# A state-space block and a top-k router on one core: another order of loads, biases and product steps at the end

## The chip, the cores and the metric

The kernel runs on one core of a Trainium2 chip. Its engines are TensorE (PE, matrix products), VectorE (DVE), ScalarE (ACT), GpSimd (POOL) and SyncE (SP); each has its own in-order instruction stream, and SP and ScalarE here also issue DMA transfers, each on a hardware queue of its own. The metric is the device time of one execution in microseconds. All data are fp32.

## The reference, cut to what matters

```python
# x (4, 1024, 1024), ctx (4, 1024, 512)
x = x + tanh(g_xattn) * mamba(ctx, layernorm(x))   # in_proj, conv of 4 taps, state scan over 1024 steps, 16 states, gate
xn = layernorm(x)
# expert-choice router: 16 experts, one shared expert matrix
S = softmax(xn @ router_w + router_b)              # (4096 tokens, 16)
G, idx = top_k(S.T, 256)                           # each expert takes its 256 best tokens
out = xn[idx] @ expert_w + expert_b                # (16, 256, 1024)
y = zeros.at[idx].add(G * out)
return x + tanh(g_ffn) * y
```

All experts use the same matrix, so a token's output is `x2 + c * (xn @ expert_w + expert_b)` with `c = tanh(g_ffn)` times the sum of the token's scores over the experts that picked it.

## The kernel before, in words

The 4096 tokens are eight halves `h` of 512 tokens (`NC = 8`), each of four tiles of 128 tokens (`TT = 4`). All engines walk through slots `g` of a half; slot tables at the top of the file say at which slot, and how many halves late, each piece of work is issued. A half's state-space part runs first; its second layer norm, logits and expert product follow in the slots of later halves. `LAST = 7`, `LATE = 6` are the two halves whose tail is left when the scans are over; `half(NC, REST)` issues the last eight slots' worth of it, after which the order is written out by hand. The parts that the change touches are these.

**Product.** `product_step` multiplies one 128x128 piece of transposed normed tokens with 512 columns of the expert matrix; eight steps make a unit (half a tile), two units a tile. The weights come in 256 KB pieces through a ring of five places (`wk`, `load_step`). When the scans are over, the space of `bbc` is free, and SP loads the whole matrix into it (`wres`, eight loads of 512 KB). The last twelve units (`units_end`: four of `LATE`, eight of `LAST`) use it, in `product_end_step(j)`, 96 steps. ScalarE copies each finished unit out of PSUM (`unit_end`). The products of tiles 0 to 25 are in DRAM (`prod_dram`), those of tiles 26 to 31 stay on chip (`product_end`), `NBACK = 26`.

**Logits at the end.** TensorE transposes the normed tokens of a tile in two groups of four (`turn_end`), ScalarE and VectorE copy them to SBUF, and `logits_end` adds up 16-column matmuls. Softmax scores of all halves lie in `S_tok`.

**Search.** The scores are transposed to 128 rows (eight halves by 16 experts) of 512. Thirty rounds find the bits of each expert's 256th largest score: VectorE counts scores over a candidate, a 128x1 matmul adds the counts of an expert's rows, VectorE decides the bit. TensorE puts one product step into each round.

**Selection.** `gtm` marks scores above the threshold, `eqm` those equal, a scan counts the equal ones (`cum`), two small matmuls sum over rows, `sele` becomes the mask times the scores, and four matmuls with `seg_of` sum it over the experts: `coef`, one factor per token.

**Draining the tiles.** For each of 32 tiles VectorE adds the bias of the expert (`biased`, 128x1024), then computes `x2 + coef * product` (`finish`); SP stores it. There are `NSLOT = 9` pairs of places for a tile of the product (`pr`) and of `x2` (`x2b`). SP fills them for tiles 0 to 8 before the search (`load_back`). Tiles 9 to 27 are loaded by ScalarE (`load_again`), two tiles after each unit from the seventh on and the others after the last unit; each load waits until the store of the place's tile before has landed. VectorE issues `biased(i + 1)` ahead of `finish(i)`.

Of the kernel before, what the change touches and what calls it, by code (L numbers as in the profile page):

```python
# [6 lines left out]
ALU = mybir.AluOpType  # L7
# [10 lines left out]
E = D // P  # L18
# [69 lines left out]

SLOTTED = 4
NRING, NPIECE = 5, 3  # L90

NSLOT = 9
NBACK = (NC - 1) * TT - 2

# [33 lines left out]
def mamba_moe(nc, x, ctxT, g_xattn, g_ffn, winT, conv_w, conv_b, xpT, dtpT, dt_b, a_log, dvec,  # L128
              router_w, router_b, expert_w, expert_b, consts, row_masks, out):
    with ExitStack() as ctx:  # L130
# [159 lines left out]
        s_sp2 = sem("selection_sums")  # L290
        s_mask = sem("masks_in")
# [7 lines left out]
        s_o1 = sem("product_biased")  # L299
        s_o = sem("tile_done")  # L300
# [47 lines left out]
        def _(sp):  # L348
# [169 lines left out]


# [4 lines left out]
            half(NC, REST)  # L524
            store_unit(LATE, SLOTTED - 1)

            def load_back(i):
                h, t = divmod(i, TT)
                sp.wait_ge(s_pw, 16 * 2 * (i + 1))
                sp.dma_start(pr[i], prod_dram[h, :, t, :]).then_inc(s_ld[i], 16)  # L530
                sp.dma_start(x2b[i], x2_dram[h, :, t, :]).then_inc(s_ld[i], 16)
# [10 lines left out]
            for i in range(NC * TT):  # L542
# [3 lines left out]
                sp.dma_start(out[h, t * P:(t + 1) * P, :], pr[slot] if i < NBACK else product_end[h][t]).then_inc(s_st[slot], 16)  # L546
            for i in range(NSLOT):
                sp.wait_ge(s_st[i], 16 * len(range(i, NBACK, NSLOT)))
# [4 lines left out]
        def _(pe):  # L553
# [93 lines left out]
            def logits_end(h, t):  # L647
                if h == LATE:

                    pe.wait_ge(s_pe, n(h, 2 * TT, SLOTTED))  # L650
# [6 lines left out]
                dst = (pM if h == LATE else pU)[:, t * NX:(t + 1) * NX]  # L657
# [38 lines left out]
            def product_end_step(j):  # L696
# [3 lines left out]
                if j == 0:  # L700
                    pe.wait_ge(s_wres, 16 * E)
                if k == 0:
# [76 lines left out]
            for t in range(1, TT):  # L779
                turn_end(LAST, 2 * t)  # L780
                turn_end(LAST, 2 * t + 1)
                logits_end(LAST, t - 1)
# [9 lines left out]

            for i in range(BITS):
                pe.wait_ge(s_b, 2 + 3 * i + 2)
                pe.matmul(pD[:, 0:1], same_expert, small[:, 0:1], start=True, stop=True).then_inc(s_cnt, 1)
                product_end_step(i)
            pe.wait_ge(s_sel, 3)
            pe.matmul(pD[:, 2:3], same_expert, small[:, 1:2], start=True, stop=True)
            pe.matmul(pD[:, 4:5], earlier, cum[:, T - 1:T], start=True, stop=True).then_inc(s_sp2, 1)
            pe.wait_ge(s_sel, 8)  # L800
            for j in range(TT):
                mm = pe.matmul(pY[:, j * NC:(j + 1) * NC], sele[:, eT(j)], seg_of, start=True, stop=True)
            mm.then_inc(s_sp2, 1)
            for j in range(BITS, len(units_end) * E):
# [3 lines left out]
        def _(act):  # L808
# [120 lines left out]
            def logits_end(h):  # L929
# [5 lines left out]
                else:  # L935
                    nc.scalar.copy(lg[:, 2:4, :].rearrange("p t s -> p (t s)"), pM[:, 2 * NX:TT * NX]).then_inc(s_lga, 2)
# [114 lines left out]
            def load_again(i):  # L1051

                h, t = divmod(i, TT)
                slot = i % NSLOT
# [426 lines left out]
```

## Time and profile before

| | |
|---|---|
| time, median of 3 runs | 2131.61 us (2131.18 to 2132.29) |
| profiled execution, its own time | 2129.65 us |
| its span, first to last instruction | 2127.5 us |
| mean granted TensorE clock | 0.88 |
| moved by DMA | 348.19 MB |

The span runs from the first to the last instruction of the profiled execution; its own time holds in addition what lies around them. Rows give start and duration in us from the span's start. L705 is line 705 of the kernel before. The granted clock is a share of the full 2.4 GHz. Tensors that share space have the name of the space: `bbc` is also the resident expert matrix, `cbc`, `states`, `u` and `sz` the places of tiles, `steps` the expert bias, `szT` the factors `coef`, `states` the masks and scores of the search.

### The profile page before, as it was taken

The numbers are of one execution on the slowest core, as the hardware profiler recorded it, in microseconds if no ns is written. First come the engines' busy times: TensorE is split into PE (matmuls) and PEld (weight loads), VectorE is DVE, ScalarE is ACT, GpSimd is POOL, SyncE is SP. The second block draws the span as 40 slices with busy tenths as digits, with TensorE's granted clock in tenths as the row PEclk, the third lists the DMA queues.
The fourth block names the chain that finished last, engine by engine and source line by source line (L and its number), as shares of the span: only waits on it lengthen the run. The fifth ranks groups of instructions, "written<-read, shape, count | busy, mean of one in ns | idle before, by whom it ended". The sixth has DMA issues, their size and how long they took to land.

```text
span 2127.5 us, 23357 instructions
## 1 busy us (share of the span) xinstructions
PE 1654.1 (78%) x7564; PEld 1082.5 (51%) x7564; DVE 1931.3 (91%) x2055; ACT 1405.6 (66%) x2115; POOL 1736.6 (82%) x758
## 2 busy tenths in 40 slices
PE   7456666678888888888878988889888778778790
PEld 2234444454555555555555555555555555556340
DVE  7988989999999899999999999999999999982667
ACT  3455756787788768786888777876888687742000
POOL 0488989998999999998999999999999999980000
PEclk9678888889999999999999988999999889886995
DMA  9600214133844465345735473537524553355088
GB/s 368 251 26 16 85 62 183 31 125 101 307 130 145 139 228 185 118 155 181 246 115 178 127 283 111 177 111 267 170 89 149 198 198 114 126 186 196 6 311 354
DMA packets 139001, 348.19 MB, mean 164 GB/s; under 512 B 15234, under 2 KB 17794, under 8 KB 129666
## 3 DMA queue, kind: packets, MB, share of 16 engines
q1 hardware_dynamic: 133698, 327.83, 44.4%
q10 hardware_dynamic: 5184, 18.88, 2.3%
q8 instruction: 61, 1.00, 0.2%
q14 instruction: 58, 0.48, 0.1%
HBM read 301.04 MB, written 45.61 MB: 163 GB/s over the span
## 4 chain that ended last, share of the span: by engine, by line
POOL 25%; PE 25%; DVE 19%; issue 15%; ACT 10%; DMA 4%; SPq 0%; DVEq 0%; POOLq 0%; ACTq 0%
POOL states L1366 15%; DVE states L1105 11%; POOL states L1354 8%; PE pY L599 7%; PE pM L693 5%; PE pA L567 4%; ACT pDec L852 4%; DVE states L1090 2%; PE pA L576 2%; DVE u L1080 2%; PE pDec L705 2%; ACT L836 1%; DMA bbc<-bc_scratch 1%; POOL dtub L1345 1%; PE pY L595 1%
## 5 line engine op out<-in xcount | busy, mean ns | idle before, releaser
L1366 POOL TENSOR_TENSOR states<-states,cbc 128x2048 f32<-128x2048 f32 x256 | 1160.5, 4536 | 32.5 <-DVE states L1105 21.8
L852 ACT ACTIVATE pDec<-steps,an 128x512 f32<-128x512 f32 x1024 | 685.1, 687 | 412.8 <-DVE states L1105 408.4
L599 PE MATMUL pY<-con,states 128*128 128x128 f32 x4096 | 587.0, 306 | 185.1 <-POOL states L1366 184.9
L599 PEld LDWEIGHTS pY<-con,states 128*128 128x128 f32 x4096 | 541.3, 160 | 303.3 <-POOL states L1366 242.1
L1105 DVE TENSOR_TENSOR_SCAN states<-pDec,carry,states 128x512 f32<-128x512 f32 x512 | 625.9, 1265 | 25.5 <-ACT pDec L852 24.9
L1105 DVE TENSOR_TENSOR_SCAN states<-pDec,states 128x512 f32<-128x512 f32 x512 | 594.8, 1204 | 37.8 <-ACT pDec L852 37.6
L1354 POOL TENSOR_TENSOR states<-dtub,bbc 128x1024 f32<-128x1024 f32 x192 | 454.3, 2366 | 63.4 <-PE pY L599 50.7
L693 PE MATMUL pM<-wk,xfT 128*128 128x512 f32 x832 | 424.6, 626 | 2.3 <-DMA wk<-in_expert_w 2.3
L1090 DVE TENSOR_TENSOR states<-pU,bbc 128x1024 f32<-128x1024 f32 x320 | 384.9, 1203 | 5.0 <-DMA bbc<-bc_scratch 3.5
L567 PE MATMUL pA<-ctx_sb,winb 128*128 128x512 f32 x448 | 228.4, 657 | 62.7 <-issue 30.1
L693 PEld LDWEIGHTS pM<-wk,xfT 128*128 128x128 f32 x832 | 148.3, 204 | 83.8 <-issue 82.2
L567 PEld LDWEIGHTS pA<-ctx_sb,winb 128*128 128x128 f32 x448 | 91.9, 211 | 184.9 <-issue 140.2
L595 PE MATMUL pY<-ddiag,u 128*128 128x128 f32 x512 | 79.1, 303 | 90.6 <-issue 73.2
L1011 ACT ACT_TABLE_LOAD x109 | 139.8, 1283 | 2.0
L595 PEld LDWEIGHTS pY<-ddiag,u 128*128 128x128 f32 x512 | 71.3, 211 | 130.5 <-issue 112.2
L1080 DVE SCALAR_TENSOR_TENSOR u<-pA,cw,u 128x509 f32<-128x509 f32 x171 | 125.1, 731 | 2.1
L1345 POOL TENSOR_TENSOR dtub<-steps,u 128x512 f32<-128x512 f32 x64 | 81.7, 1277 | 11.8 <-ACT steps L836 11.8
L836 ACT ACT_TABLE_LOAD x64 | 82.1, 1283 | 1.2
L585 PE MATMUL pD<-xpr,dtp 32*128 32x512 f32 x128 | 73.6, 655 | 11.9 <-ACT xfT L900 10.2
L610 PEld LDWEIGHTS pA<-con,sz 128*128 128x128 f32 x256 | 38.5, 168 | 63.5 <-issue 63.5
L864 ACT COPY szT<-pA 128x512 f32<-128x512 f32 x64 | 37.0, 578 | 41.6 <-PE pA L610 41.6
L1113 DVE TENSOR_TENSOR pY<-pY,szT 128x512 f32<-128x512 f32 x64 | 43.4, 678 | 22.7 <-PE pY L599 22.6
(206 smaller groups left out, 1421.5 us busy)
## 6 DMA issues: line engine op xcount, KB each, us to landing
wk<-in_expert_w SPq DMA_DIRECT2D x416, 256.0 KB, 4.3
bbc<-bc_scratch SPq DMA_DIRECT2D x32, 1024.0 KB, 7.3
cbc<-bc_scratch SPq DMA_DIRECT2D x32, 1024.0 KB, 9.4
sz<-in_x SPq DMA_DIRECT2D x34, 512.0 KB, 6.0
xt<-in_x SPq DMA_DIRECT2D x15, 1024.0 KB, 5.6
winb<-in_winT SPq DMA_DIRECT2D x58, 256.0 KB, 2.6
x_scratch<-xt SPq DMA_DIRECT2D x14, 1024.0 KB, 6.0
xr<-x_scratch SPq DMA_DIRECT2D x28, 512.0 KB, 4.0
```

What stands on the lines that cost most here:

```text
L567: mm = pe.matmul(pA[:], win[j % 2][:, part, :], ctx_sb[:, part, :], start=(part == 0), stop=(part == KC - 1))
L595: mm = pe.matmul(pY[:, eT(t)], u[h % 2][:, e, eT(t)], ddiag[:], start=(t == 0), stop=False)
L599: mm = pe.matmul(pY[:, eT(t)], states[g % NST][:, i, eT(t)], ident, start=False, stop=(q == QG - 1 and i == QN - 1 and t == TT - 1), is_tr ...
L693: pe.matmul(pM[:], piece_of(h, 2 * t + k // 4)[:, k % 4, :], wk[:, c % NRING, :], start=(k == 0), stop=(k == E - 1)).then_inc(s_moe, 1)
L836: nc.scalar.activation(dt[e % 2], pD[:], ACT.Softplus, bias=dtb[:, e:e + 1]).then_inc(s_sp, 1)
L852: nc.scalar.activation(pDec[bank_of(h, k)][:], dt[e % 2], ACT.Exp, scale=an[:, k:k + 1]).then_inc(s_dec, 1)
L1011: nc.scalar.preload_act_table_set(EXP)
L1080: nc.vector.scalar_tensor_tensor(out=dst, in0=bank[:, 0:T - HALO + i], scalar=cw[:, j, i:i + 1], in1=dst, op0=ALU.mult, op1=ALU.add).then_ ...
L1090: nc.vector.tensor_tensor(states[g % NST], spread(pU), bbc[:, QN * q:QN * (q + 1), :], ALU.mult) \
L1105: nc.vector.tensor_tensor_scan(st, pDec[bank_of(h, k)][:], st, 0.0 if h % HB == 0 else carry[:, e, k % NS:k % NS + 1], ALU.mult, ALU.add). ...
L1354: nc.gpsimd.tensor_tensor(states[g % NST], spread(dtu[e % 2]), bbc[:, QN * q:QN * (q + 1), :], ALU.mult) \
L1366: nc.gpsimd.tensor_tensor(st, st, cbc[:, QW * q:QW * (q + 1), :], ALU.mult).then_inc(s_hc, 1)
```

## The change

- SP issues only the first four of the last eight slots (`WK_REST`) before the eight loads of the expert matrix, and with them the last four small weight pieces; before, the eight loads came first.
- The logits of the last two tiles of `LATE` go to the PSUM bank `pDec[2]` and no longer wait for the copy of the unit in `pM`. The second late unit, which uses that bank, waits until they are copied.
- Six of the 96 late product steps (`EARLY = 2` after each pair of `turn_end` of tiles 1 to 3) are issued before the last logits; the search starts with the seventh.
- GpSimd adds the bias to tiles 0 to 8 as they arrive; VectorE adds it to the others only.
- Selection: the two row sums accumulate in one PSUM column; the mask above the threshold is multiplied by the scores on GpSimd, the mask of equal scores on VectorE behind the scan; both are summed by TensorE, four matmuls each.
- Loads of tiles 9 to 27 are issued by SP: after store `i`, from `i = 2` on, it waits for the landing of store `i - 2` and loads tile `i + 7`. ScalarE issues no more loads.

```diff
...
 REST = 8
+EARLY = 2
 SLOTTED = 4
+WK_REST = 4
 NRING, NPIECE = 5, 3
 NSLOT = 9
 NBACK = (NC - 1) * TT - 2
+LAG = 2
 def at(slots, g, h):
...
         s_cnt = sem("counts_summed")
         s_sel = sem("selection_step")
         s_sp2 = sem("selection_sums")
+        s_above = sem("above_threshold")
         s_mask = sem("masks_in")
         s_big = sem("expert_bias_in")
         s_wk = [sem(f"expert_ring{i}_in") for i in range(NRING)]
...
         s_pw = sem("product_written")
         s_ld = [sem(f"tile{i}_back") for i in range(NSLOT)]
         s_o1 = sem("product_biased")
+        s_o1p = sem("product_biased_pool")
         s_o = sem("tile_done")
         s_st = [sem(f"out{i}_written") for i in range(NSLOT + 1)]
...
             for h in range(NC):
                 half(h)
+            half(NC, WK_REST)
             sp.wait_ge(s_bmd, n(NC, len(DVE_GROUPS), 0))
             sp.wait_ge(s_bmp, n(NC, len(POOL_GROUPS), 0))
             for k in range(E):
                 sp.dma_start(wres[:, k, :], expert_w[k * P:(k + 1) * P, :]).then_inc(s_wres, 16)
-            half(NC, REST)
+            for g in range(WK_REST, REST):
+                side(NC, g)
             store_unit(LATE, SLOTTED - 1)
             def load_back(i):
                 h, t = divmod(i, TT)
-                sp.wait_ge(s_pw, 16 * 2 * (i + 1))
-                sp.dma_start(pr[i], prod_dram[h, :, t, :]).then_inc(s_ld[i], 16)
-                sp.dma_start(x2b[i], x2_dram[h, :, t, :]).then_inc(s_ld[i], 16)
+                slot = i % NSLOT
+                wait(sp, s_st[slot], 16 * (i // NSLOT))
+                if i < NBACK:
+                    sp.wait_ge(s_pw, 16 * 2 * (i + 1))
+                    sp.dma_start(pr[slot], prod_dram[h, :, t, :]).then_inc(s_ld[slot], 16)
+                sp.dma_start(x2b[slot], x2_dram[h, :, t, :]).then_inc(s_ld[slot], 16)
             sp.wait_ge(s_hc, n(NC, NP, 0))
...
                 sp.wait_ge(s_o, i + 1)
                 slot = i % NSLOT if i < NBACK else NSLOT
                 sp.dma_start(out[h, t * P:(t + 1) * P, :], pr[slot] if i < NBACK else product_end[h][t]).then_inc(s_st[slot], 16)
+                if i >= LAG and i - LAG + NSLOT < LAST * TT:
+                    load_back(i - LAG + NSLOT)
             for i in range(NSLOT):
                 sp.wait_ge(s_st[i], 16 * len(range(i, NBACK, NSLOT)))
             sp.wait_ge(s_st[NSLOT], 16 * (NC * TT - NBACK))
...
             def logits_end(h, t):
                 if h == LATE:
-                    pe.wait_ge(s_pe, n(h, 2 * TT, SLOTTED))
+                    pe.wait_ge(s_scan, n(NC, NU, 0))
                     pe.wait_ge(s_xfT, n(h, 2 * TT, 2 * t + 2))
                 else:
                     pe.wait_ge(s_bmd, n(NC, len(DVE_GROUPS), 0))
                     pe.wait_ge(s_xfT, n(LAST, 2 * TT, t + 1))
                     pe.wait_ge(s_xfTv, t + 1)
-                dst = (pM if h == LATE else pU)[:, t * NX:(t + 1) * NX]
+                dst = (pDec[2] if h == LATE else pU)[:, t * NX:(t + 1) * NX]
                 pe.matmul(dst, one[:], rb[:], start=True, stop=False)
                 for f in range(2):
                     piece = piece_of(h, 2 * t + f)
...
                 t, hh = divmod(i, 2)
                 if j == 0:
                     pe.wait_ge(s_wres, 16 * E)
+                if unit == 1 and k == 0:
+                    pe.wait_ge(s_lga, n(LATE, TT, TT))
                 if k == 0:
                     pe.wait_ge(s_pe, n(LATE, 2 * TT, SLOTTED + max(unit - len(p_end) + 1, 0)))
...
             for t in range(1, TT):
                 turn_end(LAST, 2 * t)
                 turn_end(LAST, 2 * t + 1)
+                for j in range(EARLY * (t - 1), EARLY * t):
+                    product_end_step(j)
                 logits_end(LAST, t - 1)
             logits_end(LAST, TT - 1)
...
             mm.then_inc(s_srt, 1)
+            first = EARLY * (TT - 1)
             for i in range(BITS):
                 pe.wait_ge(s_b, 2 + 3 * i + 2)
                 pe.matmul(pD[:, 0:1], same_expert, small[:, 0:1], start=True, stop=True).then_inc(s_cnt, 1)
-                product_end_step(i)
+                product_end_step(first + i)
             pe.wait_ge(s_sel, 3)
-            pe.matmul(pD[:, 2:3], same_expert, small[:, 1:2], start=True, stop=True)
-            pe.matmul(pD[:, 4:5], earlier, cum[:, T - 1:T], start=True, stop=True).then_inc(s_sp2, 1)
-            pe.wait_ge(s_sel, 8)
+            pe.matmul(pD[:, 2:3], same_expert, small[:, 1:2], start=True, stop=False)
+            pe.matmul(pD[:, 2:3], earlier, cum[:, T - 1:T], start=False, stop=True).then_inc(s_sp2, 1)
+            pe.wait_ge(s_above, 2)
             for j in range(TT):
-                mm = pe.matmul(pY[:, j * NC:(j + 1) * NC], sele[:, eT(j)], seg_of, start=True, stop=True)
+                pe.matmul(pY[:, j * NC:(j + 1) * NC], gtm[:, eT(j)], seg_of, start=(j == 0), stop=False)
+            pe.wait_ge(s_sel, 6)
+            for j in range(TT):
+                mm = pe.matmul(pY[:, j * NC:(j + 1) * NC], sele[:, eT(j)], seg_of, start=False, stop=(j == TT - 1))
             mm.then_inc(s_sp2, 1)
-            for j in range(BITS, len(units_end) * E):
+            for j in range(first + BITS, len(units_end) * E):
                 product_end_step(j)
         @block.scalar
...
                     act.wait_ge(s_sto, n(h, 1, 0))
                     nc.scalar.copy(lg[:].rearrange("p t s -> p (t s)"), pU[:, 0:TT * NX]).then_inc(s_lga, TT)
                 else:
-                    nc.scalar.copy(lg[:, 2:4, :].rearrange("p t s -> p (t s)"), pM[:, 2 * NX:TT * NX]).then_inc(s_lga, 2)
+                    nc.scalar.copy(lg[:, 2:4, :].rearrange("p t s -> p (t s)"), pDec[2][:, 2 * NX:TT * NX]).then_inc(s_lga, 2)
             def gate_silu(h, part):
                 wait(act, s_zx[part % 2], n(h, 32, 16 * (part // 2 + 1)))
...
             router_exp(LAST)
             scores(LAST)
-            def load_again(i):
-                h, t = divmod(i, TT)
-                slot = i % NSLOT
-                act.wait_ge(s_st[slot], 16 * (i // NSLOT))
-                if i < NBACK:
-                    nc.scalar.dma_start(pr[slot], prod_dram[h, :, t, :]).then_inc(s_ld[slot], 16)
-                nc.scalar.dma_start(x2b[slot], x2_dram[h, :, t, :]).then_inc(s_ld[slot], 16)
-            act.wait_ge(s_pw, 16 * n(LATE, 2 * TT, SLOTTED))
-            act.wait_ge(s_x2w, n(LAST, 32, 0))
-            again = iter(range(NSLOT, (NC - 1) * TT))
             for j in range(len(units_end)):
                 unit_end(j)
-                for _ in range(2 if j > 5 else 0):
-                    load_again(next(again))
-            for i in again:
-                load_again(i)
         @block.vector
         def _(dve):
...
             dve.wait_ge(s_b, 2 + 3 * BITS)
             thf = thr.bitcast(F32)
-            nc.vector.tensor_scalar(gtm, srt, thf, 0.0, ALU.is_gt, ALU.add, accum_out=small[:, 1:2])
+            nc.vector.tensor_scalar(gtm, srt, thf, 0.0, ALU.is_gt, ALU.add, accum_out=small[:, 1:2]).then_inc(s_above, 1)
             nc.vector.tensor_scalar(eqm, srt, thf, None, ALU.is_equal).then_inc(s_sel, 1)
             dve.wait_ge(s_sel, 1)
             nc.vector.tensor_tensor_scan(cum, ones, eqm, 0.0, ALU.mult, ALU.add).then_inc(s_sel, 2)
+            nc.vector.tensor_tensor(eqm, eqm, srt, ALU.mult).then_inc(s_sel, 1)
             dve.wait_ge(s_sp2, 1)
-            nc.vector.tensor_scalar(small[:, 3:4], pD[:, 2:3], -1.0, float(TOPK), ALU.mult, ALU.add).then_inc(s_sel, 1)
-            dve.wait_ge(s_sel, 4)
-            nc.vector.tensor_tensor(small[:, 4:5], small[:, 3:4], pD[:, 4:5], ALU.subtract).then_inc(s_sel, 1)
+            nc.vector.tensor_scalar(small[:, 4:5], pD[:, 2:3], -1.0, float(TOPK), ALU.mult, ALU.add).then_inc(s_sel, 1)
             dve.wait_ge(s_sel, 5)
             nc.vector.scalar_tensor_tensor(out=sele, in0=cum, scalar=small[:, 4:5], in1=eqm,
                                            op0=ALU.is_le, op1=ALU.mult).then_inc(s_sel, 1)
-            dve.wait_ge(s_sel, 6)
-            nc.vector.tensor_tensor(sele, sele, gtm, ALU.add).then_inc(s_sel, 1)
-            dve.wait_ge(s_sel, 7)
-            nc.vector.tensor_tensor(sele, sele, srt, ALU.mult).then_inc(s_sel, 1)
             dve.wait_ge(s_sp2, 2)
             nc.vector.tensor_scalar(coef, pY[:, 0:TT * NC].rearrange("p (t c) -> p t c", t=TT), tg[:, 1:2], None,
                                     ALU.mult).then_inc(s_sel, 1)
-            dve.wait_ge(s_sel, 9)
+            dve.wait_ge(s_sel, 7)
             dve.wait_ge(s_big, 16)
             def product_at(i):
...
             def finish(i):
                 h, t = divmod(i, TT)
                 slot = i % NSLOT
-                dve.wait_ge(s_o1, i + 1)
+                if i < NSLOT:
+                    dve.wait_ge(s_o1p, i + 1)
+                else:
+                    dve.wait_ge(s_o1, i + 1 - NSLOT)
                 scale = coef[:, t, h:h + 1]
                 product = product_at(i)
                 if h == LAST:
...
                                                        op0=ALU.mult, op1=ALU.add)
                 z.then_inc(s_o, 1)
-            biased(0)
             for i in range(NC * TT):
-                if i + 1 < NC * TT:
+                if NSLOT <= i + 1 < NC * TT:
                     biased(i + 1)
                 finish(i)
...
                 pool.wait_ge(s_xf, n(LATE, TT, t + 1))
                 rstd2(LAST, t)
+            pool.wait_ge(s_big, 16)
+            for i in range(NSLOT):
+                pool.wait_ge(s_ld[i], 32)
+                nc.gpsimd.tensor_tensor(pr[i], pr[i], ebias, ALU.add).then_inc(s_o1p, 1)
+            pool.wait_ge(s_above, 1)
+            nc.gpsimd.tensor_tensor(gtm, gtm, srt, ALU.mult).then_inc(s_above, 1)
 # ---- launch: one core ----
```

## Rows read from the trace of the kernel before

**Rows 1.** page head: busy us (share of span) and instructions

```profile
...
PE 1654.1 (78%) x7564; PEld 1082.5 (51%) x7564; DVE 1931.3 (91%) x2055; ACT 1405.6 (66%) x2115; POOL 1736.6 (82%) x758
```

**Rows 2.** chain of work, front and first product step: start, us, what

```profile
1902.79 10.95 DMA wk<-in_expert_w
...
1913.87 3.82 PE pM L693 x8
...
1917.71 0.59 ACT stg L919
...
1931.49 0.54 PE pU L658 x2
...
1947.78 3.54 PE pU L662 x16
...
1957.62 1.92 PE pM L705 x2
```

**Rows 3.** chain of work, selection

```profile
2010.92 0.24 PE pD L799 x2
...
2013.07 0.70 DVE states L1293
...
2013.82 1.88 PE pY L802 x8
```

**Rows 4.** timeline of VectorE and of SP's queue, drain; in brackets idle before

```profile
2016.02 2.36 DVE L1312 TENSOR_TENSOR cbc<-cbc,steps 128x1024 f32<-128x1024 f32 x2
...
2019.60 7.33 SPq L546 DMA_DIRECT2D out<-cbc  x4
...
2045.24 1.23 DVE L1312 TENSOR_TENSOR cbc<-cbc,steps 128x1024 f32<-128x1024 f32 x1 [9.35 <-DMA cbc<-x_scratch]
...
2106.26 1.23 DVE L1312 TENSOR_TENSOR u<-u,steps 128x1024 f32<-128x1024 f32 x1 [1.64 <-DMA u<-x_scratch]
...
2124.40 0.33 SPq L546 DMA_DIRECT2D out<-dtub  x1
```

**Rows 5.** timeline of ScalarE's queue, its first tile loads

```profile
2039.52 0.34 ACTq L1057 DMA_DIRECT2D cbc<-product_scratch  x1
...
2040.86 0.45 ACTq L1058 DMA_DIRECT2D cbc<-x_scratch  x1
```

**Rows 6.** windows: us, busy of the engines, PEclk, DMA share, GB/s

```profile
1925.00:1930.00 5.00, 5.00 (x24) 4.63 (x23) 0.69 (x1) 0.70 (x4) 0.00 (x0) 0.50 0.99 351
...
2032.00:2040.00 8.00, 8.00 (x20) 3.61 (x19) 3.89 (x4) 1.07 (x2) 0.00 (x0) 1.00 0.48 197
...
2088.00:2096.00 8.00, 0.00 (x0) 0.00 (x0) 5.92 (x6) 0.00 (x0) 0.00 (x0) 0.50 1.03 420
```

**Rows 7.** timeline of TensorE, front

```profile
1911.00 0.60 PE L621 MATMUL pD<-con,xr 128*128 128x128 f32 x4
...
1918.67 1.96 PE L662 MATMUL pM<-rw,xfT 128*128 128x16 f32 x16
...
1926.11 3.60 PE L662 MATMUL pM<-rw,dtub 128*128 128x16 f32 x16
```

**Rows 8.** transfers of the tile stores, from issue to landing

```profile
DMA to landing us min/median/max: 2.6/4.0/8.2
```

**Rows 9.** windows of TensorE alone: us, busy, PEclk, DMA share, GB/s

```profile
1924.00:1951.00 27.00, 27.00 (x122) 0.50 0.88 341
...
1957.00:1963.00 6.00, 5.96 (x12) 0.50 0.00 0
...
1964.00:2008.00 44.00, 35.43 (x106) 1.00 0.00 1
```

**Rows 10.** costliest groups on the page, GpSimd's multiplies

```profile
L1354 POOL TENSOR_TENSOR states<-dtub,bbc 128x1024 f32<-128x1024 f32 x192 | 454.3, 2366 | 63.4 <-PE pY L599 50.7
...
L1345 POOL TENSOR_TENSOR dtub<-steps,u 128x512 f32<-128x512 f32 x64 | 81.7, 1277 | 11.8 <-ACT steps L836 11.8
```

**Rows 11.** DMA queues on the page: packets, MB, share; q10 is ScalarE's

```profile
q10 hardware_dynamic: 5184, 18.88, 2.3%
```

## The prediction

> **What bounds the kernel now.** I read the profile from the end backwards. The head of the page gives a span of 2127.5 us, with VectorE at 91% and GpSimd at 82% busy over the whole [rows 1]; the diff alters nothing that runs before about 1897 us, so only the last 230 us matter. For these I read the chain of work, the timelines of single engines and busy time by window. The reader is to see four stretches.
>
> Front, to 1951.3 us: the chain runs through TensorE. It waits for the piece of expert weights that SP issued at 1902.79, behind the eight large weight loads, and that landed at 1913.74; then for ScalarE's copy of the finished unit; then it alternates transposes and logits until 1951.3 [rows 2]. Search, 1957 to 2008: thirty rounds between VectorE and TensorE. Selection, 2008 to 2016: a serial chain that ends in the group sums [rows 3]. Drain, from the first store at 2019.60 to the end: VectorE works at its own pace until the nine tiles that are on chip are used up, then stands 9.35 us for the tenth [rows 4]. ScalarE issues that load only at 2039.52, because in its program the load stands behind the seventh unit of the late product [rows 5]. The windows show the price: 197 GB/s at half the transfer engines' time before 2040, 420 GB/s once loads and stores run together [rows 6]. At the very end VectorE is again what is late: from the bias of tile 25 at 2106.26 it never stops, and the last store goes out at 2124.40 [rows 4].
>
> **The change, part by part.**
>
> *Order of the weight loads.* With WK_REST = 4 the last four small pieces go out ahead of the eight large ones. TensorE then need not stop between the transposes that end at 1911.60 [rows 7] and the steps that start at 1913.87 [rows 2]: 2.3 us. Three of the pieces are still issued only when their places in the ring come free (about 1906.8 to 1908.8), but into an empty queue; there 512 KB land in 2.6 us [rows 8] and 256 KB should not need more, and a step takes 3.82/4 = 0.95 us [rows 2], so they keep ahead. The large loads move to about 1909; 4.2 MB at 400 GB/s take 10 us, so they are in near 1921, before the first early step at 1928.6. The two loads and eighteen tile loads behind them on SP then end near 1945, 70 us ahead of their use. The logits of the late half's third tile no longer wait for the copied unit (1917.69 to 1918.3 [rows 2]): 0.6 us. Together 2.9 us. Should the pieces come late after all, up to these 2.3 us are lost.
>
> *Early product steps.* Six steps move into the front, two behind each of three pairs of transposes, and all lie on the path. At the lower level (granted clock 0.50, 1.2 GHz) a step takes 1.92 us [rows 2]: 11.5 us, so the front would end at 1951.3 - 2.9 + 11.5 = 1959.9, 8.6 us later than now. But now the stretch runs at the lower level from end to end, with TensorE never idle for 27 us on transposes and matmuls of 16 columns [rows 9], and a logits group takes 3.60 us there against 1.96 at the upper level, 2.4 GHz [rows 7]. If the first two steps raise the clock, they end at 1931.5 - 2.9 + 3.8 = 1932.4; the 19.8 us of transposes and logits after 1931.5 shrink by 1.96/3.60 to 10.8, and four steps at 0.95 take 3.8: end 1947.0, 4.3 us earlier than now. In the search the first steps start at 1957.6 at 0.50, and from 1964 on the clock is 1.00 although TensorE idles a fifth of the time [rows 9]: 512-column steps do raise and hold it. A pair of transposes with two steps is 5.6 us without a pause, so I expect a rise at the first or the second pair, with perhaps one relapse in a logits group. I take 2.0 us earlier than now, near the favourable end, since the search is the nearest row; -4.3 and +8.6 stay as bounds. That the late product ends five us sooner is worth nothing: its first tile is used last but five.
>
> *GpSimd's nine biases.* A GpSimd multiply of the same size takes 2.37 us [rows 10], the tile loads come every 2.5 us and end near 1945, so the last bias ends near 1948, under TensorE's front and before the search. Without that cover 21 us of GpSimd would lie beside the search.
>
> *Selection.* The two small matmuls still end at 2011.16 [rows 3]; the new product of the equal mask hides under them. VectorE's path loses a 128x1 step and two passes of 0.70 us. But the group sums double: 1.88 us for each mask, so 2011.16 + 2 x 1.88 = 2014.9 against 2015.7, and TensorE takes over: 0.8 us gained at that pace. At half that time for each (the upper level, as in the logits) the second mask, ready near 2012.2, is later than TensorE: end 2013.1, gain 2.6. I take 1.0, near the observed pace. GpSimd's multiply of 128x512 takes 1.28 us [rows 10] and ends near 2010.1, before its sum is due.
>
> No row has a GpSimd multiply beside a VectorE instruction with two inputs on chip, as it would now be for the scan. The nearest, the main loop, keeps both engines busy 82% and 91% [rows 1], which speaks for nothing as the price; the other bound is the whole 1.28 us. The Trainium skill, "SBUF — State Buffer", "SBUF: two separate sides", speaks against the change here: the ports that the two engines share are locked for a whole instruction, and whoever comes second waits. By it the scan starts some 1.2 us late and the selection gains nothing; no row of before decides it.
>
> *First store.* Two biases (2.36 us with the launch between them [rows 4]) leave VectorE's path ahead of the first finish: 2.3 us. The first store goes out at 2019.6 - 2.0 - 1.0 - 2.3 = 2014.3.
>
> *Drain.* A tile of 512 KB is 0.524 MB: 1.25 us at 420 GB/s. There are 32 stores and 36 loads (the second queue's 18.88 MB [rows 11]), 68 transfers. Now SP alone issues them: store i, then, once store i - 2 has landed, the two loads for tile i + 7. Behind SP's wait stands the next store, which nobody but SP waits for while places are loaded ahead. When the wait ends, six transfers stand in the queue, 7.5 us of work, and SP needs 0.34 to 0.45 us for an issue [rows 5]; the queue does not run dry. VectorE needs 2.35 us for a tile's bias and finish, the transfers 3 x 1.25 = 3.75. So tile 25 is in after 19 stores and 34 loads: 53 x 1.25 = 66.2, plus a fixed 1.4 (the landing of 2.6 [rows 8] less 1.25) is 67.6 us after the first store. From the bias of tile 25 on, VectorE's order stays: now 2106.26 to the last issue at 2124.4, 18.1 us, and 3.1 us to the end [rows 4]. Sum 88.8 us, against 107.9 now. The transfers' own floor, 68 x 1.25 + 1.4 = 86.4, is close below.
>
> End: 2014.3 + 88.8 = 2103.1, which is 24.4 us under the profiled span of 2127.5. That execution took 2129.65 us in all, 2.0 less than the median of 2131.61; I take the difference off the median: **2107.2 us**.
>
> **Rivals.**
>
> *The clock stays down in the front* although steps are added. For: 27 us at 0.50 with no idle time [rows 9]. Against: there were no 512-column matmuls in it. Price 8.6 + 2.0 = 10.6 us: 2117.8. Chance 0.15.
>
> *One queue with loads and stores mixed carries less.* For: tile loads alone on SP's queue moved 351 GB/s at a share of 0.99 for 5 us [rows 6]. Against: two queues mixed held 420. At 351 a transfer takes 1.49 us and the floor sets the end: 68 x 1.49 + 1.4 = 102.7, span 2117.0, time 2121.1. Chance 0.10. The Trainium skill, "DMA: Bandwidth & Descriptors", "Specifications", puts the HBM limit of a core at about 358 GB/s; by it this rival would be nearly certain, but the window at 420 exceeds it, and the measurement decides.
>
> *Slower: SP stands in its waits for landings.* From the fourth store on, three stores go out per landing time L plus about 0.95 us of issues; in the full queue L is 3 x 3.75 - 0.95 = 10.3. To lose all 24.4 us over the 19 waits a tile must take 1.28 more, 5.03 us, so this decides from L = 14.1 us on. For: no row shows stores behind loads in one full queue. Against: stores never took over 8.2 us [rows 8], and six transfers behind each wait limit the depth. At L = 15 a tile takes 5.32 us, 29.8 us more than forecast: 2137. Chance 0.05.
>
> *The shared ports hold the selection up.* 2.2 us at most with the gain gone: 2109.4, inside the forecast's own range; of the forecast's chance 0.2 is this one's.
>
> **How the numbers follow.** Forecast 0.66 in all (own range 2103, with the front at -4.3 and the selection at 2.6, to 2112, with two pairs at the lower level or 400 GB/s); clock down 0.15; weaker queue 0.10; slower 0.05; an end that moves by less than 10 us for another reason 0.04. The range reaches from 2102 over the clock rival to 2119. A measurement of this kernel tells about 0.2%, 4.3 us, from no change: faster 0.93, same 0.02, slower 0.05.
>
> **What the profile after would show.** TensorE busy from 1911.6 to 1915; a clock of 1.00 in windows between 1930 and 1946; last logits near 1949; GpSimd's ninth add over by 1950; the first store near 2014; windows of 420 GB/s from 2020 to 2080; the bias of tile 25 68 us after the first store, and 18 us of unbroken VectorE behind it. A front that ends after 1955, drain windows under 400 GB/s, or stores that land after 14 us would prove it wrong.

## The result, and the profile after

The kernel after takes 2105.29 us (2104.57 to 2105.98, four runs) against 2131.95 (2131.18 to 2133.0) for the kernel before beside it: a ratio of 0.9875, 95% interval 0.9857 to 0.9892. Forecast were 2107.2 us in a range of 2102 to 2119. The profiled execution has a span of 2103.7 us; the sum had given 2103.1. The terms were less exact than that: the front gained more than was taken, the selection gained nothing in this profile, and the drain is longer than forecast.

I cut both traces at the same events. All lengths are differences of starts or ends in the timelines, in us. Each row runs from the event of the row above it to its own; "ring" is the product that still takes its weights from the ring of five places.

| stage | before | after | forecast change | measured |
|---|---|---|---|---|
| up to the end of the last scan | 1901.9 | 1901.0 | 0 | -0.9 |
| to the copy of the last unit of the ring | 15.8 | 14.5 | -2.3 | -1.3 |
| to the last half's first transposes | 6.0 | 5.2 | -0.6 | -0.7 |
| to the copy of the last logits | 27.7 | 25.8 | +0.9 | -1.9 |
| to the first count of the search | 4.8 | 4.8 | 0 | 0.0 |
| search, to the mask of equal scores | 52.4 | 52.1 | 0 | -0.4 |
| selection, to coef | 7.3 | 7.5 | -1.0 | +0.2 |
| to the first store | 3.6 | 1.4 | -2.3 | -2.3 |
| to the bias of tile 25 | 86.7 | 70.3 | -19.1 | -16.4 |
| to the issue of the last store | 18.1 | 18.2 | 0 | 0.0 |
| to the end | 3.1 | 3.0 | 0 | 0.0 |

The forecast of the fourth row is what was taken for the six early steps and the clock together: the stage was to start 2.9 us earlier than before and to end 2.0 us earlier. The last scan ends at 1901.0 to 1906.6 in the executions of this study, although no kernel differs before it. That is why small effects are read from stages below and not from medians. Each stage is one profile of one execution, and some of them vary too, as the second profile of the kernel after shows below.

Chain of work of the kernel after, the same pieces as [rows 2], then the selection as [rows 3]:

```profile
1912.06 3.44 PE pM L709 x8
...
1928.58 2.83 PE pM L724 x4
1931.41 0.32 PE pU L674 x2
1931.73 1.89 PE pU L678 x16
...
1943.63 2.85 PE pU L678 x16
...
2006.77 0.43 PE pD L821 x2
2007.19 1.72 PE pY L824 x8
2008.91 1.72 PE pY L827 x8
```

The four ring steps now follow the transposes at once; the wait for a weight piece and the wait for the copy are gone. The first two early steps take 2.83 us, less than two at 1.92, because the clock rises inside them, at 1930.7. It falls again at 1944.3, inside the last group of logits, which takes 2.85 us where the groups before it take 1.89. Windows of the kernel after, as [rows 6] (busy time of PE, PEld, DVE, ACT and POOL, then clock, share and GB/s):

```profile
1925.00:1930.00 5.00, 5.00 (x19) 4.04 (x19) 1.31 (x4) 3.09 (x10) 0.59 (x1) 0.50 1.02 410
1930.00:1935.00 5.00, 5.00 (x31) 3.73 (x30) 0.43 (x1) 2.68 (x7) 3.71 (x2) 0.93 1.03 411
1935.00:1940.00 5.00, 5.00 (x31) 3.58 (x30) 0.84 (x2) 0.59 (x1) 4.61 (x3) 1.00 1.02 408
1940.00:1945.00 5.00, 5.00 (x33) 4.08 (x32) 0.11 (x1) 0.00 (x0) 4.58 (x3) 0.93 1.02 409
...
2012.00:2020.00 8.00, 8.00 (x15) 3.40 (x14) 8.00 (x8) 0.59 (x1) 0.00 (x0) 0.75 0.87 280
...
2036.00:2044.00 8.00, 8.00 (x20) 3.61 (x19) 4.84 (x4) 0.59 (x1) 0.00 (x0) 1.00 1.03 419
```

Where [rows 9] showed 0.50 throughout, the clock is up from the first pair of steps into the last logits. The first two windows of the drain carry 280 and 395 GB/s, those from 2028 on 417 to 420, until the last transfers.

Timelines of VectorE, GpSimd and SP's queue in the kernel after, selection and drain, as [rows 4]:

```profile
2003.61 1.44 POOL L1440 TENSOR_TENSOR states<-states 128x512 f32<-128x512 f32 x1 [50.38 <-DVE states L1286]
...
2004.03 2.09 DVE L1289 TENSOR_TENSOR_SCAN states<-states 128x512 f32<-128x512 f32 x1
...
2012.25 2.72 SPq L560 DMA_DIRECT2D out<-cbc  x3
2015.08 0.40 SPq L544 DMA_DIRECT2D cbc<-product_scratch  x1
...
2021.98 1.23 DVE L1315 TENSOR_TENSOR cbc<-cbc,steps 128x1024 f32<-128x1024 f32 x1 [1.38 <-DMA cbc<-x_scratch]
...
2082.51 1.23 DVE L1315 TENSOR_TENSOR u<-u,steps 128x1024 f32<-128x1024 f32 x1 [1.36 <-DMA u<-x_scratch]
```

The first load goes out 2.8 us after the first store, before it was 19.9 us. VectorE's wait for tile 9 is 1.38 us in place of 9.35, and it then waits about 1.37 us for every tile: the transfers set the pace, one tile in 3.78 us. Stores now land later, as the full queue makes them (kernel after, issue to landing of the stores, answering to [rows 8]):

```profile
DMA to landing us min/median/max: 2.6/9.8/10.5
```

### The profile page after: what moved, and what is told of

Read it like the earlier page. It is cut to its first block, busy times and chain, and to the rows that moved or that the text cites. A ratio compares the mean times of both kernels' runs of the same rounds, so it can differ in the third digit from the quotient of the medians.

```text
span 2103.7 us, 23390 instructions
## 1 busy us (share of the span) xinstructions
PE 1648.5 (78%) x7572; PEld 1075.5 (51%) x7572; DVE 1921.0 (91%) x2044; ACT 1405.7 (67%) x2115; POOL 1759.3 (84%) x768
## 4 chain that ended last, share of the span: by engine, by line
POOL 27%; PE 24%; DVE 18%; issue 16%; ACT 10%; DMA 5%; SPq 0%; DVEq 0%; POOLq 0%; ACTq 0%
POOL states L1371 16%; DVE states L1113 10%; POOL states L1359 9%; PE pY L615 7%; PE pM L709 4%; PE pA L583 4%; ACT pDec L877 3%; PE pA L592 2%; DVE states L1098 2%; DVE u L1088 2%; ACT L861 1%; PE pY L611 1%; POOL dtub L1350 1%; DMA bbc<-bc_scratch 1%; ACT L1036 1%
```

## The experiments

There are twelve runs, of edits of the kernel after or of that kernel itself. Their ratios are to the kernel before on the same chip; the kernel after stands at 0.9875 [0.9857, 0.9892]. Of all intervals only that of the loads on ScalarE lies clear of this one, and that of LAG = 1 all but clear. The other edits are read from stages.

**The clock in the front: no early steps.**

```diff
-EARLY = 2
+EARLY = 0
```

> The changed kernel with no product step between the last logits (EARLY = 0); all 66 remaining steps run later, as before. Theory (the steps raise TensorE's clock and so pay for themselves): the front stays at a granted clock of 0.50 from about 1923 us to its end, which comes at 1951.3 - 2.9 = 1948.4 us against 1946.5 in the changed kernel; one more slow round in the search adds 0.4 us: 2.3 us slower than the changed kernel, about 2107.6 us. Rival (the clock would have risen anyway, and the six steps are only work on the path): the front shows 1.00 in its second half and ends 5 us or more before 1946.5, about 2100 us.

Measured: 2107.49 us (2106.85 to 2109.16), ratio 0.9883 [0.9866, 0.9899]. Windows of this kernel's TensorE (busy, clock, share, GB/s):

```profile
1925.00:1930.00 5.00, 5.00 (x24) 0.50 1.03 412
1930.00:1935.00 5.00, 5.00 (x25) 0.50 1.03 410
1935.00:1940.00 5.00, 5.00 (x24) 0.50 1.03 409
1940.00:1947.00 7.00, 7.00 (x33) 0.50 1.03 410
```

The stage to the last logits is 27.7 us without the steps and 25.8 with them, although they are 5 us of work even at the upper level. The rival falls. The search was 0.4 us shorter here, not longer (51.7 us), and the selection took 6.5 us: which rounds and sums meet the lower level changes from run to run.

**One step in place of two.**

```diff
-EARLY = 2
+EARLY = 1
```

> The changed kernel with one product step behind each of three pairs of transposes (EARLY = 1). Theory (uninterrupted work with 512-column matmuls raises the clock; pairs of transposes plus one step are 3.7 us at the lower level against 5.6): a rise is less sure and may come a pair later; if it comes at the first pair, the front ends some 3 us before the changed kernel's, otherwise up to 1 us after it. Rival (the clock rises only with both steps): 0.50 to the end of the front, which ends 1.9 - 0.4 = about 2 us plus 3 x 1.9 us later than with one rise, at some 49 us after the last scan.

Measured: 2107.06 us (2102.69 to 2109.11), ratio 0.9879 [0.9863, 0.9896]. The clock:

```profile
1925.00:1930.00 5.00, 5.00 (x23) 0.50 1.03 410
1930.00:1935.00 5.00, 5.00 (x20) 0.56 1.03 412
1935.00:1940.00 5.00, 5.00 (x39) 1.00 1.03 407
1940.00:1947.00 7.00, 7.00 (x46) 0.83 1.03 410
```

One step for each pair raises the clock too, and the stage falls to 23.8 us. The rival falls: the rise came 1.9 us after the first single step began. The search was 53.1 us in this execution, but it was 53.0 in the kernel after beside it as well; the time does not tell the two kernels apart.

**The order of the weight loads undone.**

```diff
-WK_REST = 4
+WK_REST = 0
```

> The changed kernel with the eight large weight loads ahead of the last four small pieces again (WK_REST = 0). Theory: TensorE waits 2.3 us near 1912 us for a piece, and everything after it shifts: 2107.6 us. Rival (the shift is swallowed, because ScalarE's norm of the last half or the clock sets the front's end): within 0.5 us of the changed kernel's 2105.3 us.

Measured: 2109.61 us (2108.24 to 2112.79), ratio 0.9893 [0.9876, 0.9911]. TensorE of this kernel waits again:

```profile
1914.45 3.81 PE L709 MATMUL pM<-wk,xfT 128*128 128x512 f32 x8 [2.02 <-DMA wk<-in_expert_w]
```

In the kernel after the same steps start at 1911.90 without idle time and take 3.60 us. So the order is worth 2.0 us of waiting and 0.2 us of pace, as forecast (2.3). The median is 4.3 us above that of the kernel after, on another chip and with overlapping intervals; 2.4 us of the difference between the profiles lie before the end of the last scan.

**Who issues the loads.**

```diff
-                if i >= LAG and i - LAG + NSLOT < LAST * TT:
-                    load_back(i - LAG + NSLOT)
...
             for j in range(len(units_end)):
                 unit_end(j)
+                for _ in range(2 if j > 5 else 0):
+                    load_again(next(again))
+            for i in again:
+                load_again(i)
```

> The changed kernel with the loads of tiles 9 to 27 issued by ScalarE behind the late units again; all else as changed. Theory (the drain gained because the loads start with the stores): the seventh unit is done near 2029 us, ten us sooner than in the kernel before, so the first load goes out then, and the end follows 88 us later as it did before: 2117 us span, about 2119 us, some 14 us slower than the changed kernel; VectorE idles some 6 us for tile 9. Rival (the transfers set the end anyway and the gain came from front, biases and selection): 2105 to 2108 us.

Measured: 2121.48 us (2119.68 to 2123.9), ratio 0.9948 [0.993, 0.9966]. Its VectorE, and its first load on ScalarE's queue:

```profile
2033.12 0.34 ACTq L1079 DMA_DIRECT2D cbc<-product_scratch  x1
...
2038.39 1.23 DVE L1328 TENSOR_TENSOR cbc<-cbc,steps 128x1024 f32<-128x1024 f32 x1 [15.21 <-DMA cbc<-x_scratch]
```

The first load went out at 2033, not at 2029 as I had worked out, and VectorE stood 15.2 us, not 6: with nine tiles biased in advance it used them up by 2023. From the first store to the bias of tile 25 it is 84.5 us against 70.3. This one move carries 14.2 us of the gain, and it is where the sooner load shows: two queues or one made no difference in the full stretches, which carry 418 to 420 GB/s here too.

**Who adds the first nine biases.**

```diff
+            biased(0)
             for i in range(NC * TT):
-                if NSLOT <= i + 1 < NC * TT:
+                if i + 1 < NC * TT:
...
-            for i in range(NSLOT):
-                pool.wait_ge(s_ld[i], 32)
-                nc.gpsimd.tensor_tensor(pr[i], pr[i], ebias, ALU.add).then_inc(s_o1p, 1)
```

> The changed kernel with the bias of tiles 0 to 8 added by VectorE again, in its old place in the drain; GpSimd adds none. Theory: the first store goes out 2.3 us later (two biases ahead of it), the queue fills just as fast afterwards, since a tile's three transfers take 3.75 us and its two VectorE passes 2.35: 2.3 us slower, about 2107.6 us. Rival A (VectorE's pace in the first nine tiles limits the queue too): 4 us or more slower, 2109 or above. Rival B (the drain is set by transfers alone): under 0.5 us.

Measured: 2110.74 us (2108.71 to 2111.76), ratio 0.9893 [0.9874, 0.9913]. Rival A holds, and the theory had only its first half: the first store comes 2.3 us later (3.6 us after coef against 1.4), and from there to tile 25 it takes another 2.2 us (72.5 against 70.3). The transfer engines of this kernel in half-microseconds from 2012 on (busy tenths, GB/s) show why:

```profile
DMA  0000000000995039920699797996889999999999
GB/s 0 0 0 0 0 0 0 0 0 0 393 434 221 0 123 418 426 82 0 254 401 352 148 197 205 279 238 197 246 295 369 385 410 418 401 434 385 410 434 426
```

At one store in 2.3 us the queue is empty between stores until loads join. The biases thus carry 4.5 us, of which the prediction had 2.3.

**The scan beside GpSimd's multiply.**

```diff
+            dve.wait_ge(s_above, 1)
+            nc.vector.tensor_tensor(gtm, gtm, srt, ALU.mult).then_inc(s_above, 1)
...
-            pool.wait_ge(s_above, 1)
-            nc.gpsimd.tensor_tensor(gtm, gtm, srt, ALU.mult).then_inc(s_above, 1)
```

> The changed kernel with the mask above the threshold multiplied on VectorE behind the scan, not on GpSimd beside it. Theory (the scan and GpSimd's multiply hold each other up at shared ports): the scan takes 1.24 us again, as in the kernel before, not 2.10, and coef comes some 0.9 us sooner: about 2104.4 us. Rival (the scan is longer for another reason, such as the bias adds or the matmuls around it): it stays at 2.1 us and the kernel at 2105.3 us or above.

Measured: 2105.73 us (2103.43 to 2107.24), ratio 0.9872 [0.9855, 0.9889]; the time can't tell it from the kernel after. The profile can:

```profile
2006.33 1.22 DVE L1289 TENSOR_TENSOR_SCAN states<-states 128x512 f32<-128x512 f32 x1
```

The scan is back from 2.09 to 1.22 us, and the selection from 7.5 to 6.6 us with TensorE's group sums at the same 1.85 us each. So the longer scan came from GpSimd: it took 2.09 or 2.10 us in each of the eleven profiles with the multiply beside it, whatever the clock, and 1.22 or 1.23 in the two of edits without it.

**How deep the queue must be.**

```diff
-LAG = 2
+LAG = 1
```

> The changed kernel with LAG = 1: after store i SP waits for the landing of store i - 1 and loads tile i + 8. Theory (the queue does not run dry): at the end of each wait three transfers, 3.75 us of work, still stand behind, more than the 1.4 us until the landing is seen plus 0.9 us of issues; windows stay near 418 GB/s and the time within 1 us of 2105.3 us. Rival (SP's waits need the depth of six): windows under 400 GB/s and 4 us or more slower.

Measured: 2116.27 us (2109.01 to 2120.24), ratio 0.9916 [0.9892, 0.9941]. The profiled execution, the one of 2109.01, carried 408 GB/s from 2040 to 2080 and needed 93.3 us from the first store to the end, the other three executions took 7 to 11 us more in all. A second profile was to show where:

> The kernel with LAG = 1 once more, for a second profile. Its first profile showed windows of 408 GB/s with single dips, 93 us from the first store to the end, and three other executions of it took 5 to 9 us longer than the profiled one. Theory (with three transfers behind each wait the queue is at the edge: whenever two loads and a store land late together, it runs dry): windows under 400 GB/s in the drain and first store to end 95 us or more in a slow execution. Rival (the spread lies in the main loop, not in the drain): first store to end 93 us again, whatever the total.

Measured: 2119.71 us in one execution. Its windows in the drain:

```profile
2032.00:2048.00 16.00, 16.00 (x38) 7.04 (x38) 10.02 (x9) 1.76 (x3) 0.00 (x0) 1.00 1.00 383
...
2064.00:2080.00 16.00, 2.74 (x7) 0.95 (x5) 7.43 (x7) 0.59 (x1) 0.00 (x0) 0.65 0.98 330
2080.00:2096.00 16.00, 0.00 (x0) 0.00 (x0) 7.88 (x7) 0.00 (x0) 0.00 (x0) 0.50 0.96 320
```

First store to end is 103.6 us, and the drain is where the time is lost. The transfer engines still count as busy at a share of 0.96 to 0.98 while they carry 320 to 330 GB/s. So my theory for LAG = 1 failed: the five executions with three transfers behind a wait took 2109 to 2120 us, although the engines are hardly ever idle by the busy share. Why they carry less then, the trace does not show.

```diff
-LAG = 2
+LAG = 4
```

> The changed kernel with LAG = 4: loads of tile i + 5 after store i. Theory: deeper queue, the same 418 GB/s, and the same total; the stores alone keep the queue busy at the start, so it ends within 1 us of 2105.3 us, with stores landing after some 18 us. Rival (a later first load leaves VectorE without a tile, as before the change): an idle stretch of VectorE over 3 us for tile 9 and 2 us or more slower.

Measured: 2110.43 us (2108.04 to 2111.15), ratio 0.9891 [0.9875, 0.9907]. The rival holds:

```profile
2026.25 1.23 DVE L1315 TENSOR_TENSOR cbc<-cbc,steps 128x1024 f32<-128x1024 f32 x1 [4.25 <-DMA cbc<-x_scratch]
```

The full windows carry the same 418 GB/s, but VectorE waits 4.25 us for tile 9, and tile 25 comes 2.7 us later. The queue did not get deeper either: the stores landed after 8.9 us in the median, not the 18 of the theory, and SP waited for VectorE's tiles and for no landing before the end. LAG = 2 lies between the two losses.

**VectorE's part of the tail.**

```diff
+                if k == E - 1:
+                    if unit == 0:
+                        pe.wait_ge(s_big, 16)
+                    mm = pe.matmul(bank[:], one[:], ebias[0:1, hh * 512:(hh + 1) * 512], start=False, stop=True)
...
-                if NSLOT <= i + 1 < NC * TT:
+                if NSLOT <= i + 1 < NBACK:
```

> The changed kernel with the bias of tiles 26 to 31 added in PSUM by a one-row matmul at the end of each late unit, so that VectorE has no bias pass left for them. Theory (in the last 18 us VectorE, not the queue, is late): VectorE's work from tile 25 on falls from 18.1 to 11.3 us, the fifteen transfers left need 18.8 us and now set the end; 2.4 us faster than the changed kernel, about 2102.9 us, windows near 418 GB/s to within 4 us of the end. Rival (the queue alone sets the end already): within 0.5 us of 2105.3 us.

Measured: 2109.33 us (2107.69 to 2109.99), ratio 0.9887 [0.9871, 0.9902]: no gain. The tail did as the theory said, VectorE's part from tile 25 on fell from 18.2 to 11.6 us, and the queue was full up to the end:

```profile
2080.00:2102.00 22.00, 0.00 (x0) 0.00 (x0) 15.34 (x17) 0.00 (x0) 0.00 (x0) 0.50 1.03 420
```

But first store to end fell only from 91.4 to 90.5 us, and the search grew from 52.1 to 56.4. Four units end inside the search, and there the added matmul stands ahead of the next count; the clock also fell to its lower level in two stretches, from 1973.6 to 1977 and from 2001 to 2004:

```profile
1970.51 1.12 PE L730 MATMUL pDec<-steps,one 1*128 1x512 f32 x2
...
1973.48 1.91 PE L725 MATMUL pDec<-bbc,dtub 128*128 128x512 f32 x2
```

**The kernel after again, and two edits together.** The two kernels ran side by side:

> The changed kernel itself, unedited, to be timed beside the next three on the same chip. In the runs so far the time at which the main loop ends moved by up to 4 us between executions, so stages are compared by their lengths: front from the end of the last scan to the last logits' copy 44.3 us (45.6 where GpSimd's last multiply came late), search 52.1, selection 7.5, first store to end 91.4. Expected: these again, and a median between 2105 and 2110 us.

> The changed kernel with two edits: the mask above the threshold multiplied on VectorE, and the bias of tiles 28 to 31 alone added by a one-row matmul in units that all end after the search. Theory: the search stays at 52.1 us (the bias matmuls lengthened it only because four units end inside it), selection 6.6 us where TensorE's clock is low, VectorE's work from tile 25 on falls to 13.6 us, the queue sets the end 90.5 us after the first store: 1.8 us faster than the unedited changed kernel beside it. Rival (the search was longer for TensorE's clock alone, whatever the bias matmuls): search at 54 us or above and no gain.

```diff
+                biased_here = k == E - 1 and h == LAST
...
+                    mm = pe.matmul(bank[:], one[:], ebias[0:1, hh * 512:(hh + 1) * 512], start=False, stop=True)
...
+            nc.vector.tensor_tensor(gtm, gtm, srt, ALU.mult).then_inc(s_above, 1)
...
-                if NSLOT <= i + 1 < NC * TT:
+                if NSLOT <= i + 1 < LAST * TT:
...
-            nc.gpsimd.tensor_tensor(gtm, gtm, srt, ALU.mult).then_inc(s_above, 1)
```

The kernel after: 2106.2 us (2105.48 to 2108.31), ratio 0.9877 [0.986, 0.9893]. With both edits: 2104.95 us (2103.1 to 2105.39), ratio 0.987 [0.9855, 0.9885]. The intervals overlap.

The second profile of the kernel after was not what I had expected of its stages: the search took 53.0 us, not 52.1, and the selection 6.5, not 7.5, although the scan took 2.09 us again. TensorE of this execution in the selection:

```profile
2010.02 1.04 PE L824 MATMUL pY<-states 128*128 128x8 f32 x8
...
2011.20 1.88 PE L827 MATMUL pY<-states 128*128 128x8 f32 x8
```

The clock was still at its upper level in the group sums of the first mask, 1.04 us against 1.85 in the first profile (1.72 in its chain, which leaves the overlap out), and fell before those of the second. The kernel without early steps shows the same, with 6.5 us. So the selection of one and the same kernel takes 7.5 or 6.5 us, by when the clock falls; the comparison of 7.5 with 6.6 us under the scan above holds because there the clock was down for both masks, with GpSimd's multiply and without.

With both edits the search takes 52.1 us, the selection 6.6 with both masks at the lower level, and first store to end 90.5 us, where the kernel after has 91.4 and 91.6 in its two profiles. That a search with no added matmul keeps its 52.1 us speaks for the theory, though the unedited kernel's 53.0 shows how far a single profile carries. I count this version as no slower and about 1 us better in its drain, not as shown faster by its time.

## Why the prediction was right, point by point

*Order of the weight loads*, forecast 2.9 us with the copy's wait. Right: undoing the order cost 2.2 us on TensorE's own path, and the stage behind it is 0.7 us shorter in the kernel after. The two stages together fell by only 2.0 in the first pair of profiles, because the stage from the last scan varies from 12.6 to 14.6 us between executions of the same code.

*Early steps*, taken as 0.9 us of cost, bounds -1.4 to +11.5 on the stage. The rise came at the first pair and the one relapse only inside the last group of logits, so the stage fell by 1.9 us, half a microsecond beyond the favourable bound. The mechanism is shown by the kernel without the steps, at 0.50 to its end; all profiles with steps show the rise. What was taken was too cautious by 2.8 us. The rival "the clock stays down" is out.

*GpSimd's nine biases.* They ended at 1953.2, not 1948, and the last one lay beside the first rounds of the search; the counts there still took 0.74 us, so nothing was lost. Their worth was undersized: 4.5 us, not 2.3, since VectorE's old pace also left the queue half empty.

*Selection*, forecast -1.0, measured +0.2 in the first profile of the kernel after and -0.8 in the second. The step that failed inside a forecast that held is the price of GpSimd beside a scan with two inputs on chip. I had taken 0, from a main loop that never has that pair; it costs 0.86 us, in every profile. GpSimd's multiply started first and took 1.44 us where another of its size takes 1.28 [rows 10], and the scan ended late. The Trainium skill, "SBUF — State Buffer", "SBUF: two separate sides", had said that the later of the two blocks. The trace agrees: the multiply lay over the first 1.0 us of the scan, which took 2.09 us against 1.23, and 1.22 again once VectorE multiplies. The rival stood in the prediction with the right mechanism at up to 1.2 us, and with too small a chance. That the second profile comes close to the forecast all the same is luck: there the clock stayed up for the first mask, which the forecast had not counted on, and paid for the scan.

*First store*, forecast 2014.3, was 2012.25: the two biases gave 2.3 us as forecast; front, main loop and search were 3.2 us better than taken and the selection 1.2 worse.

*Drain*, forecast 88.8 us, measured 91.4. Pace and landing were right: a tile in 3.78 us against 3.75, stores landing after 9.8 us in the median against 10.3, the tail 18.2 against 18.1. What was missing is a term at the start: tile 25 came 70.3 us after the first store, not 67.6, of which the pace explains about half a microsecond. From 2016.5 to 2021, once the first load was in the queue, it carried 139 to 311 GB/s, with the transfer engines busy to nine tenths in six of the nine half-microseconds and to five or more in the others. The kernel before has the same dip when its loads start, 113 to 287 GB/s for 1.6 us, and all edits have it, with one queue or two and at every LAG. At 418 GB/s the same bytes would have taken 2 us less; the cause stays open.

*Rivals.* One queue carries less: no, 418 GB/s against 420 with two queues. The Trainium skill's 358 GB/s per core ("DMA: Bandwidth & Descriptors", "Specifications") is exceeded by both; the Trainium skill has that figure as one core's share of a memory stack that two cores use, and here one core ran, so it did not make this rival nearly certain, as the prediction says. SP standing in its waits: not at LAG = 2. At LAG = 1 SP does wait for landings in every round while less is carried; whether its waits are the cause is not shown.

First store and drain fit together: they gained 2.3 + 16.4 = 18.7 us, and the two edits that undo the move of the loads and the nine biases give back 14.2 and 4.5.

The span's end hit the forecast within 1 us (2103.7 against 2103.1) by luck in the sizes: terms off in both directions cancel, front 1.9, main loop 0.9 and search 0.4 us better, selection 1.2 and drain 2.6 us worse. The mechanism of each large term was right. The time, in turn, came 1.9 us below its forecast, because the forecast had put the profiled execution 2.0 us under the median, as before the change; after it, it lay 0.5 us above.

## What to carry to other kernels

Ask of each load which instruction stands ahead of it in its issuer's program: here the loads were not slow, they stood behind matrix products that had nothing to do with them, and moving them gave 14 of 27 us. Read the depth that a queue has left when its issuer's wait ends, and try it rather than trust a sum: six transfers of 512 KB kept the rate, three did not, though by the sum they should have. Work added to a path on TensorE can pay for itself where the granted clock is at the lower level, and work added to a round that was just balanced, as in the search, can cost more than its own length. Before a stage of one profile is compared with one of another, look whether the clock was the same in both.

## What the runs showed of the hardware that was not expected

- TensorE was busy without a pause for 27 us on transposes and logits matmuls at a granted clock of 0.50 (1.2 GHz). With product steps behind the first pair of transposes, two or only one, it rose to 1.00 (2.4 GHz) 1.7 to 3.0 us after the first of them began (kernel after in two profiles, the kernel with one step, the one with the old order of loads).
- When the tile loads joined the stores in the queue, it carried 139 to 311 GB/s for some 4 us, with the transfer engines busy for most of it, before it reached 418.
- With only three transfers behind each wait the same traffic ran at 408 GB/s from 2040 to 2080 in one execution and at 320 to 383 in three windows of another, with the engines busy at 0.96 or more in these.
- A scan over 512 columns took 2.09 us beside a GpSimd multiply and 1.22 us alone; the search's counts took 0.74 us beside a bias add on GpSimd as without it.
- The granted clock fell before the group sums of the selection in one execution of a kernel and between them in another, and moved the stage by 0.9 us (7.5 and 6.5).
